# Gated cross-attention block with a routed FFN: halves of queries and keys from PSUM, reciprocals in PSUM, other routing operations, other order of the projections, loops written out

## What is computed

```python
x = x + tanh(g_xattn) * attn(layernorm(x), ctx, ctx)   # 16 heads of 16, one causal block of 128 per sequence
x = x + tanh(g_ffn)   * ffn(layernorm(x))
# attn: q = (xn wq^T + bq) / 4;  k = ctx wk^T + bk;  v = ctx wv^T + bv
#       out = softmax(causal(q k^T)) v;  out wo^T + bo
# ffn:  xn = layernorm(x) * gamma + beta;  probs = softmax(xn Wr^T);  the best 2 of 8 experts
#       rank of a token in its expert, by token order; ranks from 640 on are dropped
#       y = W3 (silu(g) * u), (g, u) = W12 xn;  out += y * prob
```

## Time and profile before

| | us |
|---|---|
| median of 3 runs | 534.14 (533.56 to 534.17) |
| the profiled execution, its own time | 534.19 |
| its span, first to last instruction | 532.3 |

### The profile page before, as it was taken

The page is one execution under the profiler, slowest core; times in us unless marked ns, Lnnn a source line. Parts: engine busy times, 40 slices in busy tenths (PEclk is TensorE's granted clock), DMA queues, the critical chain, the costliest instruction groups (busy, mean ns, idle before and its releaser), DMA issues.

```text
span 532.3 us, 10749 instructions
## 1 busy us (share of the span) xinstructions
PE 479.7 (90%) x3551; PEld 444.7 (84%) x3551; DVE 360.8 (68%) x854; ACT 298.9 (56%) x757; POOL 208.9 (39%) x272
## 2 busy tenths in 40 slices
PE   5699999899999877369998999999999999999991
PEld 4588887777877666269998999999999999999991
DVE  6867888988888997547876574485843768544240
ACT  3689878677778764416664564373723747423230
POOL 8636776787787566510212012203032030311202
PEclk9999999999999997779999999999999999999996
DMA  8868432314142611153677362347451474201111
GB/s 269 209 140 250 78 41 72 75 57 81 42 80 55 205 42 53 58 175 118 234 184 219 78 226 34 60 129 193 132 144 20 130 188 131 31 4 17 13 19 20
DMA packets 41649, 57.33 MB, mean 108 GB/s; under 512 B 3721, under 2 KB 38576, under 8 KB 39552
## 3 DMA queue, kind: packets, MB, share of 16 engines
q1 hardware_dynamic: 35168, 48.62, 31.7%
q0 software_dynamic: 6144, 8.07, 9.1%
q10 hardware_dynamic: 288, 0.00, 0.0%
HBM read 36.24 MB, written 16.72 MB: 99 GB/s over the span
## 4 chain that ended last, share of the span: by engine, by line
PE 55%; DVE 3%; issue 2%; POOL 1%; DMA 0%; ACT 0%; POOLq 0%; DVEq 0%
PE bank L1438 17%; PE bank L1440 17%; PE bank L1439 17%; PE bank L1432 2%; PE bank L1361 1%; PE bank L1304 1%; POOL expert_rows L484 0%; DMA expert_rows<-xr,slotu 0%; DVE pT L929 0%; PE bank L1290 0%; POOL out_tokens L546 0%; DVE nm L924 0%; PE bank L1231 0%; PE bank L1238 0%; DVE osum L938 0%
## 5 line engine op out<-in xcount | busy, mean ns | idle before, releaser
L546 POOL DMA_INDIRECT out_tokens<-ysc,rows x32 | 49.6, 1550 | 245.6 <-DVE ysc L1142 238.9
L1438 PE MATMUL bank<-bXh,wh 128*128 128x384 f32 (+1 forms) x384 | 122.1, 318 | 2.9 <-issue 2.6
L1440 PE MATMUL bank<-bXh,wl 128*128 128x384 f32 (+1 forms) x384 | 121.8, 317 | 0.0
L1439 PE MATMUL bank<-bXl,wh 128*128 128x384 f32 (+1 forms) x384 | 121.8, 317 | 0.0
L749 ACT ACTIVATE sil<-bank 128x384 f32<-128x384 f32 (+1 forms) x96 | 43.7, 456 | 128.4 <-PE bank L1440 127.2
L1121 DVE TENSOR_TENSOR hF<-sil,bank 128x384 f32<-128x384 f32 (+1 forms) x96 | 48.9, 510 | 77.9 <-ACT sil L749 71.3
L633 ACT ACTIVATE p<-bank,nm 128x128 f32<-128x128 f32 x256 | 73.6, 387 | 14.7 <-DVE nm L924 14.7
L1438 PEld LDWEIGHTS bank<-bXh,wh 128*128 128x128 f32 x384 | 72.7, 189 | 3.3 <-issue 3.3
L1438 PE MATMUL bank<-wh,hH 128*128 128x256 f32 x256 | 73.8, 288 | 0.3 <-DVE ysc L1142 0.3
L1439 PEld LDWEIGHTS bank<-bXl,wh 128*128 128x128 f32 x384 | 72.7, 189 | 0.0
L1440 PEld LDWEIGHTS bank<-bXh,wl 128*128 128x128 f32 x384 | 72.6, 189 | 0.0
(11 more groups left out here) (146 smaller groups left out, 878.8 us busy)
## 6 DMA issues: line engine op xcount, KB each, us to landing
stage<-in_w12T SPq DMA_DIRECT2D x16, 1024.0 KB
stage<-in_w3T SPq DMA_DIRECT2D x8, 1024.0 KB
expert_rows<-padrow SPq DMA_DIRECT2D x8, 662.5 KB, 7.9
rows<-expert_rows SPq DMA_DIRECT2D x7, 662.5 KB, 4.4
kM<-k SPq DMA_DIRECT2D x64, 64.0 KB, 2.4
cT<-in_ctxT SPq DMA_DIRECT2D x8, 256.0 KB, 3.1
out_tokens<-x_all SPq DMA_DIRECT2D x8, 256.0 KB, 2.3
x_all<-in_x SPq DMA_DIRECT2D x2, 640.0 KB, 8.5
```

The costliest lines, as they stand in the source:

```text
L546: pool.indirect_dma_start(out=out, out_offset=bass.IndirectOffsetOnAxis(rows[par][:, c, D + E:ROW].bitcast(U32), 0), in_=ysc[par][:, c, :] ...
L1438: nc.tensor.matmul(out_ap, ah, bh, start=start, stop=False)
L1439: nc.tensor.matmul(out_ap, ah, bl, start=False, stop=False)
L1440: return nc.tensor.matmul(out_ap, al, bh, start=False, stop=stop)
```

## The change

- **Queries and keys.** `qT` and `kT` go. ACT writes the high half straight from PSUM (two instructions each). DVE takes the low half from PSUM, (bank + bias) - high, in two instructions each for keys and queries, at g = 1 and g = 3. The scale of the queries moves into the copy of the transposed input.
- **Order of the projections.** Keys at g = 0, `input_columns` at g = 1, queries at g = 2, values at g = 4. `input_columns` waits until DVE has taken the low half of the keys from `Xp`. ACT's steps follow; `values1` is at g = 5, `values2` at g = 7.
- **POOL.** No `keys_low` and `queries_low`. `values_rest` and `values_third` of block n+1 both stand in body n, ahead of `dispatch`; `normalize_inputs` moves ahead of the layer norms.
- **Reciprocals.** `orec` lies in PSUM, in the last columns of the bank that holds the weighed values.
- **Routing.** `expert_probs` goes, the gate columns come from one instruction. `member` keeps all 16 sequences and the ranks are counted by PE from all of them, with a start per expert; `seen`, `seen_add` and `slot0` go, `slots` has four instructions in place of seven. The rank products move to the end of g = 7. The last count takes 16 products in place of one.
- **Start.** ACT zeroes one half of `kM` 0, which was two instructions of DVE.
- **Loops.** The loops over bodies are written out on all engines.

```diff
+        orec = [O[i][:, 8 * VW:8 * VW + 8] for i in range(2)]
@@ SyncE
-                sp.wait_ge(pool_kl, n + 1)
+                sp.wait_ge(dve_kl, n + 1)
...
-            sp.wait_ge(km_zero[0], 4)
+            sp.wait_ge(km_zero[0], 3)
...
-            with sp.Fori(1, NSB // 2 - 1) as i:
+            for i in range(1, NSB // 2 - 1):
@@ GpSimd
                 if cur:
-                    values_third(n, par)
                     residual(n, par, prev1)
-                if nxt:
-                    keys_low(n + 1)
+                if nxt2:
+                    normalize_inputs(n + 2)
                 if prev1:
                     norm2(n - 1, 0)
                     if cur:
                         normalize2(n - 1, 1 - par, 0, reuse)
-                if nxt2:
-                    normalize_inputs(n + 2)
                 if nxt:
-                    queries_low(n + 1, 1 - par)
+                    values_rest(n + 1, 1 - par)
                 if prev1:
                     norm2(n - 1, 1)
                     if cur:
                         normalize2(n - 1, 1 - par, 1, reuse)
                 if nxt:
-                    values_rest(n + 1, 1 - par)
+                    values_third(n + 1, 1 - par)
                 if prev2 and cur:
                     token_numbers(n - 2, par)
                     dispatch(n - 2, par)
@@ ScalarE
-                act.activation(xT[:, :, :], Xp[:, :].rearrange("p (c t) -> p c t", c=DC), ACT.Copy).then_inc(act_xT, 1)
+                act.activation(xT[:, :, :], Xp[:, :].rearrange("p (c t) -> p c t", c=DC), ACT.Copy, scale=HD ** -0.5).then_inc(act_xT, 1)
...
+            def keys(n, bank):
                 act.wait_ge(pe_k, n + 1)
...
+                for t in range(DC):
+                    act.activation(k2[:, 0, t, :], bank[:, t * SB * T:(t + 1) * SB * T], ACT.Identity, bias=bqkv[:, 1, t:t + 1])\
+                       .then_inc(act_kh, 1)
...
+                    if cur:
+                        exps(G, g, not prev1 and g < 2)
+                    if g == 0 and nxt:
+                        keys(n + 1, Xp)
+                    elif g == 1 and nxt:
+                        input_columns(n + 1)
+                    elif g == 2 and nxt:
+                        queries(n + 1, 1 - par, Xp)
+                    elif g == 4 and nxt:
+                        values(n + 1, Xp)
+                    elif g == 5 and nxt:
+                        values1(n + 1, 1 - par)
+                    elif g == 7 and nxt:
+                        values2(n + 1, 1 - par)
...
+            act.activation(kM[0][:, 1, :, :].rearrange("p h (a t) -> p (h a) t", t=P),
+                           ident32[:, :].unsqueeze(1).to_broadcast([P, 2 * H, P]), ACT.Copy, scale=0.0).then_inc(km_zero[0], 1)
@@ VectorE
             def gate_columns(m, mpar):
-                dve.wait_ge(dve_r, R_CHAIN * m + 4)
-                dve.tensor_scalar(xr[mpar][:, :, D:D + E], prob[:, :, :], tg[:, 1:2], None, ALU.mult).then_inc(dve_wp, 1)
+                dve.wait_ge(dve_r, R_CHAIN * m + 3)
+                dve.scalar_tensor_tensor(xr[mpar][:, :, D:D + E], lex[:, :, :], tg[:, 1:2], lrc[:, :].unsqueeze(2).to_broadcast([P, SB, E]),
+                                         ALU.mult, ALU.mult).then_inc(dve_wp, 1)
...
-                dve.tensor_scalar(late[:, :, :], rk, float(CAP), LATE, ALU.is_ge, ALU.mult).then_inc(dve_rk, 1)
-                dve.tensor_tensor(slot0[:, :, :], rk, ebase[:, :].unsqueeze(1).to_broadcast([P, SB, E]), ALU.add).then_inc(dve_rk, 1)
-                dve.tensor_reduce(seen_add[:, :], member[:, :, :].rearrange("p j e -> p e j"), AX_X, ALU.add).then_inc(dve_rk, 1)
+                dve.tensor_tensor(late[:, :, :], rk, limit[:, :].unsqueeze(1).to_broadcast([P, SB, E]), ALU.is_ge).then_inc(dve_rk, 1)
...
-                dve.tensor_tensor(slot[:, :, :], slot0[:, :, :], late[:, :, :], ALU.add).then_inc(dve_rk, 1)
-                dve.tensor_tensor(seen[:, :], seen[:, :], seen_add[:, :], ALU.add)
...
+                dve.scalar_tensor_tensor(slot[:, :, :], late[:, :, :], LATE, rk, ALU.mult, ALU.add).then_inc(dve_rk, 1)
...
+            def keys_low(n, bank):
+                dve.wait_ge(act_kh, DC * (n + 1))
+                for t in range(DC):
+                    ins = dve.scalar_tensor_tensor(k2[:, 1, t, :], bank[:, t * SB * T:(t + 1) * SB * T], bqkv[:, 1, t:t + 1],
+                                                   k2[:, 0, t, :].bitcast(F32), ALU.add, ALU.subtract)
+                ins.then_inc(dve_kl, 1)
...
                     if cur:
                         largest(G, g)
+                    if g == 1 and nxt:
+                        keys_low(n + 1, Xp)
+                    elif g == 3 and nxt:
+                        queries_low(n + 1, 1 - par, Xp)
@@ TensorE
                 if not first:
-                    pe.wait_ge(act_vf, n)
+                    pe.wait_ge(dve_kl, n + 1)
...
+                for j in range(first):
+                    nc.tensor.matmul(rk, onesb[:, :], member[:, j, :].unsqueeze(1).to_broadcast([P, SB, E]), start=False, stop=False)
...
                     if nxt:
-                        if g == 2:
+                        if g == 0:
                             keys(n + 1, 1 - par, Xp, use)
+                        elif g == 1:
+                            input_columns(n + 1, False, not prev1)
+                        elif g == 2:
+                            queries(n + 1, Xp)
                         elif g == 4:
-                            queries(n + 1, Xp)
-                        elif g == 6:
-                            pe.wait_ge(act_q32, DC * (n + 2))
+                            pe.wait_ge(dve_ql, n + 2)
                             values(n + 1, 1 - par, Xp)
...
+                    if g == 7 and prev2:
+                        pe.wait_ge(dve_x2, SB * n)
+                        ranks(n - 2, Xo)
```

More of the change, by code:

```diff
@@ L683, in _ @@
             body(1, 1, True, False, True, True)
-            with act.Fori(1, NSB // 2 - 1) as i:
+            for i in range(1, NSB // 2 - 1):
                 body(2 * i, 0, True, True, True, True)
@@ L1032, in _ @@
             body(1, 1, True, True, True, True, True)
-            with dve.Fori(2, NSB // 2 - 1) as i:
+            for i in range(2, NSB // 2 - 1):
                 body(i, 0, True, True, True, True, True)
@@ L1383, in _ @@
             body(3, 1, True, True, True, True, True, 3)
-            with pe.Fori(2, NSB // 2 - 1) as i:
+            for i in range(2, NSB // 2 - 1):
                 body(2 * i, 0, True, True, True, True, True, i + 1)
```

148 lines of the change are left out of this document (53 added, 95 removed).

## The result

The change makes the kernel slower: 550.81 us (median of four runs, 546.83 to 552.65) against 534.06 us of the kernel before on the same chip, a ratio of 1.031 (95% interval 1.025 to 1.036). Forecast were 532.4 us, with 537.6 as the upper end. The profiled execution took 550.61 us, 548.9 of it its span: 16.6 us more than before.

What follows compares the result with a forecast made beforehand. The first part was taken as bound by a loop over DVE, POOL and PE, 24.33 us a body. Terms -0.8 + 2.4 - 0.5 + 0.4 - 2.4 - 0.9 = -1.8 took 534.19 to 532.4 us; 8-in-10 range 528.0 to 537.6.

Steps and rivals of the forecast that it cites:

- The second part moves in time and keeps its length: Second part, the experts: the change touches only the first part, so the second part's length changes by 0.
- The loops' jumps: Rival, looped bodies: each had cost half a microsecond in jumps that shows in no row; 531.4 us, chance 0.04.
- POOL leaves the loop: Bodies: POOL makes the values a scoring stage before PE asks; work queued behind `dispatch` is wanted much later, cost nothing.
- The new loop: Bodies 3 to 6: DVE, a step over ACT, then PE set the pace, 24.42 us against 24.33; four bodies +0.4 us.
- D: DVE's time from group 5's largest scores to those of the next group 0: 10.48 us before, 8.84 forecast, ends 8.5 and 9.6.
- the step over ACT: New loop, group 0's largest scores, exponentials, high half of the keys, then DVE's low half: 3.45 us.
- PE's part: New loop, PE from `input_columns` to the end of group 5's scores: 12.13 us, mostly read from body 2.
- Bodies 1 and 2: A new PE wait at `input_columns`, 1.2 us each, +2.4 us; body 2 no longer waits for `member`, -0.5 us.
- Body 7 and the tail: Body 7 loses a blocked head-scaling product and PE's wait for the values, -2.4 us; shorter DVE work behind it, -0.9 us.
- Start: Start and body 0: the keys' spread begins earlier, and body 0's wait at `input_columns` gives about half back: -0.8 us.
- The sign: Whole kernel, chances of the outcome: faster 0.50, same 0.18, slower 0.32.
- the four rivals: Slower loop 536.6 us (0.27), earlier loop 528.4 (0.20), reciprocals in PSUM not freeing the product 538.6 (0.05), jumps 531.4 (0.04).

Runs made afterwards that it cites:

- the run with plain transfers: Changed kernel with POOL's indirect transfers of the routed rows replaced by plain ones to fixed rows; single execution, body 5 loses 0.5 and body 6 1.6 us.
- the run with ACT's loop: Changed kernel with ACT's attention loop alone made a loop again, the other engines' left written out: 548.92 us, ratio 1.020 to the kernel before.
- the looser order: Changed kernel with input transposes, queries and values one group later each (groups 2, 3, 5), keys still at group 0: 538.72 us, ratio 1.004 to the kernel before.

## Why the prediction was wrong

- **"The second part moves in time and keeps its length": failed, +7.1 us.** It has the same instructions and not the same length, since PE's added products move its code. The row was there: before has one wait of 2.61 us at the third expert, and I took it for part of that length without asking what it was. "The loops' jumps" looked for such a cost only in the looped bodies, where writing out indeed changes nothing; the cost of jumps lies in the branches of the second part.
- **"POOL leaves the loop", "I cost that at nothing": half failed.** The waits for the third part of the values are gone. But the indirect transfers of `dispatch` hold up the signals of the other engines, and in the new loop PE, ACT and DVE pass each group on to one another over these signals. That was so before the change, too: in body 5 `dispatch` begins at 136.70, 6.2 us behind the first scores (145.00 and 6.9 us after), and ACT starts 1.91 us behind the start of PE's transposes at its end, against 0.63 to 0.74 in bodies 0 to 3:

```profile
140.47 0.60 PE L1276 MATMUL bank<-ident,p 128*128 128x128 f32 x4
142.38 0.60 ACT L640 ACTIVATE pT<-bank 128x512 f16<-128x512 f32 x1 [1.20 <-PE bank L1276]
```

  There the loop ran over POOL, and PE waited for POOL until 142.83 in any case. I looked only for who is queued behind `dispatch` on POOL. By the run with plain transfers it comes to 0.5, 1.6 and, by the reckoning for the clock, 1.5 us in bodies 5, 6 and 4.
- **The new loop: found, and two of its three terms rightly sized.** The terms, in place of the earlier trace rows, can be read in bodies 5 and 6 of the changed kernel:

```profile
158.15 0.69 DVE L893 TENSOR_REDUCE nm<-bank 128x4 f32<-128x512 f32 x1 [0.16 <-PE bank L1251]
166.89 0.68 DVE L893 TENSOR_REDUCE nm<-bank 128x4 f32<-128x512 f32 x1
169.51 0.88 DVE L930 SCALAR_TENSOR_TENSOR k<-bank,bqkv,k 128x256 fp32r<-128x256 f32 x2 [0.24 <-ACT k L583]
170.53 0.63 PE L1180 MATMUL bank<-ident,xn 128*128 128x128 f32 x4 [1.56 <-DVE k L930]
184.44 0.69 DVE L893 TENSOR_REDUCE nm<-bank 128x4 f32<-128x512 f32 x1 [0.16 <-PE bank L1251]
```

  D is 166.89 - 158.15 = 8.74 us (8.84 forecast), the step over ACT 170.39 - 166.89 = 3.50 (3.45), and PE's part 184.44 - 170.39 = 14.05 (12.13). The term that failed is PE's: I took it from body 2 as if PE ran through, and it waits 1.43 us in it for the logits' input. ACT's order has a part in that: the copy of the routed rows, which stood ahead of the exponentials of its group, now stands behind them and behind the queries, so a late signal reaches the logits later. No run changes that order alone. With plain transfers the loop is 24.65 us, 0.23 over the forecast. Four bodies came to +5.1 in place of +0.4.
- **Bodies 1 and 2: the right wait, too small a price.** PE waits 1.22 us at `input_columns` in each, 1.2 forecast, yet they are 1.8 and 1.9 us longer. The step left out, in body 1, 0.18 us for ACT's copy of the output's columns, and in body 2, 0.32 us for the context load and 0.31 us for DVE's low half of the probabilities; the 0.4 us for `member` went, as forecast. The rest, 0.4 us in each, is PE's own busy time (20.90 us in place of 20.53, and 22.36 in place of 21.97).
- **Body 7 and the tail: right in sign, too large.** The product that scales the heads (L917; L948 in the earlier trace rows) takes 288 ns on average, and PE no longer waits for POOL. Of the 2.4 us in body 7 0.7 came, of 0.9 in the tail 0.4. What is next in body 7 is more than the half microsecond that I took: PE stands 1.25 us there for ACT's copy of the output's columns and 0.98 us (0.8 before) for DVE's low half of the probabilities. `pslot` (L883), which reads two SBUF tiles, now takes 727 ns in place of 192. The Trainium skill ("SBUF — State Buffer", Who interferes with whom) says that a DVE instruction with two SBUF inputs contends with a GpSimd instruction that reads SBUF. The row agrees.
- **Start: failed by the clock.** The spread begins at 11.13 us, as forecast, but the first scores come 0.5 us earlier, not 1.5, since PE's own queue ahead of them is later (the queries at 12.67 in place of 11.67). Body 0 waits 3.19 us at `input_columns`, and I priced that wait, but not what follows it: the fall of the clock to 1.2 GHz. In the run with ACT's loop the clock stayed at 2.4 GHz. There body 0 takes 20.26 us (19.65 before the change) and body 1 begins at 38.18 us, 0.5 earlier than before, near the forecast of 0.8. So the clock is the miss here, and it doesn't fall in every execution.
- **The sign.** I gave the slower side 0.32, nearly all of it through D. D was right, and none of the four rivals names what happened. Of the 18.4 us between the forecast's -1.8 and the measured +16.6, the length of the second part makes 7.1 and the late signals some 3.7, both of them places where I had put a zero.

## What to carry to other kernels

A part whose code isn't edited can still change its time: compare the waits at its branches, and the instruction queue's packets at them, before and after, and price a shift of the code at what one such wait costs. When an order puts the only wait on a step one group behind the work it waits for, give it a second group; here that was 11 us in eight bodies, about 1.4 of it the clock in body 0. When a change moves the loop that sets the pace to other engines, look for what already delays those engines without cost: the indirect transfers ran at the same place in the body before, and their late signals lay beside PE's wait for POOL.

## What the runs showed of the hardware that was not expected

- A taken branch near the beginning of a 16 KB block of PE's code costs 2.5 to 4.7 us in this kernel, and then often 1.5 to 1.8 us more at a lower granted clock. With 26 products that compute nothing the whole kernel is 0.45% faster.
- While POOL issues indirect transfers, other engines get on late: DVE 1.7 to 4.2 us behind PE's scores in place of 1.1 (from 1.71 in body 5 of the changed kernel to 4.16 in body 5 of the looser order), and small products of PE without a wait between them come in steps of 0.7 or 1.4 us. The first set, in body 3, brings none of that. With plain transfers the lag is 1.1 us, but for body 4, where the clock fell. By what path they do that is open.
- Right behind a wait of PE its granted clock can fall to 0.50 (1.2 GHz), and that costs 1.3 to 1.8 us more: in body 0 of the changed kernel behind 3.19 us (25.0 to 28.5 us), in body 3 of three runs made from the kernel before behind 1.35 to 1.46 us. It is not so in every execution: the same wait of 1.35 us in body 3 of the kernel before (until 94.31), and its 2.61 us at the third expert, brought no fall.
